# Row maxima turned on VectorE instead of TensorE, in a fused cross-attention and FP4 feed-forward kernel

## What is computed

```python
def reference(x, ctx_512, g_xattn, g_ffn, Wq, Wk, Wv, Wo, bo, w_gate, w_up, w_down):
    qh = (layernorm(x) @ Wq)      # (B, 16, N, 64)
    kh, vh = ctx_512 @ Wk, ctx_512 @ Wv
    attn = softmax(qh @ kh.T * 64 ** -0.5)
    x = x + tanh(g_xattn) * ((attn @ vh) @ Wo + bo)
    z = fp4(layernorm(x))
    h = silu(z @ fp4(w_gate).T) * (z @ fp4(w_up).T)
    return x + tanh(g_ffn) * (fp4(h) @ fp4(w_down).T)
```

## Time and profile before

| | us |
|---|---|
| median of 3 runs | 548.04 (547.64 to 551.53) |
| profiled execution | 547.66 |
| its span, first to last instruction | 545.8 |
| TensorE busy in it | 532.4 |
| VectorE busy | 439.2 |
| ScalarE busy | 312.8 |
| GpSimd busy | 279.9 |

### The profile page before, as it was taken

One profiled execution on the slowest core, in us unless ns is written; L12 is line 12 of the kernel. 1 busy time (PEld: TensorE's weight loads), 2 busy tenths in 40 slices (PEclk: granted clock), 3 DMA queues, 4 the chain that ended last, 5 costly groups with the idle time before them and its releaser, 6 DMA issues.

```text
span 545.8 us, 8243 instructions
## 1 busy us (share of the span) xinstructions
PE 532.4 (98%) x2769; PEld 319.8 (59%) x2769; DVE 439.2 (80%) x765; ACT 312.8 (57%) x724; POOL 279.9 (51%) x260
## 2 busy tenths in 40 slices
PE   7989999999999999999999999999999999999997
PEld 4655656656565665656566565756556565655553
DVE  5868889798887979798887978789786988877865
ACT  4365546765467556765467645665567654555611
POOL 4046294745629463574927465383826566184300
PEclk9999999999999999999999999999999999999999
DMA  7502001110012100020011100120000200000000
GB/s 186 114 1 56 0 1 31 29 27 2 1 34 37 19 1 28 9 55 0 2 29 35 28 0 2 36 54 1 1 28 4 29 1 1 5 0 1 2 4 4
DMA packets 10017, 12.28 MB, mean 23 GB/s; under 512 B 4144, under 2 KB 7736, under 8 KB 9976
## 3 DMA queue, kind: packets, MB, share of 16 engines
q1 hardware_dynamic: 9000, 8.85, 6.6%
q0 software_dynamic: 560, 2.59, 3.2%
q10 hardware_dynamic: 416, 0.33, 0.2%
HBM read 11.35 MB, written 0.41 MB: 22 GB/s over the span
## 4 chain that ended last, share of the span: by engine, by line
PE 91%; DVE 6%; issue 2%; ACT 1%; POOL 0%; DVEq 0%; ACTq 0%; POOLq 0%
PE attn L931 28%; PE scores L914 19%; PE ring L840 13%; PE scores L915 12%; PE ring L857 5%; PE ring L850 4%; PE ring L820 3%; DVE max L1071 2%; PE ring L863 2%; PE ring L871 1%; PE ring L843 1%; PE attn L887 1%; ACT q_hh L638 1%; DVE e_gate L1025 0%; PE ring L799 0%
## 5 line engine op out<-in xcount | busy, mean ns | idle before, releaser
L749 ACT ACTIVATE probs<-scores 120x400 f32<-120x400 f32 (+1 forms) x384 | 185.5, 505 | 158.5 <-PE scores L915 156.1
L1071 DVE TENSOR_REDUCE max<-ring 116x1 f32<-116x482 f32 (+2 forms) x336 | 203.5, 651 | 58.2 <-PE ring L840 56.7
L592 POOL TENSOR_TENSOR acc_p<-acc_p,probs 120x800 f32<-120x800 f32 x75 | 145.2, 1936 | 64.2 <-ACT probs L749 59.9
L931 PE MATMUL attn<-probs,ctx_n 120*64 120x400 f32 (+1 forms) x768 | 170.2, 524 | 0.6 <-ACT probs L749 0.6
L914 PE MATMUL scores<-q_hh,k_hl 128*120 128x400 f32 (+1 forms) x384 | 154.6, 402 | 1.2 <-DVE q_ls L1075 0.7
L914 PEld LDWEIGHTS scores<-q_hh,k_hl 128*120 128x120 f32 (+1 forms) x384 | 69.6, 181 | 125.1 <-ACT probs L749 89.5
L915 PE MATMUL scores<-q_ls,k_h 71*120 71x400 f32 (+1 forms) x384 | 133.0, 346 | 0.0
L840 PE MATMUL ring<-k_hl,q_hh 128*116 128x482 f32 (+2 forms) x336 | 111.9, 403 | 1.9 <-DVE q_ls L1053 0.7
L915 PEld LDWEIGHTS scores<-q_ls,k_h 71*120 71x120 f32 (+1 forms) x384 | 70.3, 183 | 3.8
L931 PEld LDWEIGHTS attn<-probs,ctx_n 120*64 120x64 f32 (+1 forms) x768 | 38.3, 134 | 53.6 <-issue 33.5
L840 PEld LDWEIGHTS ring<-k_hl,q_hh 128*116 128x116 f32 (+1 forms) x336 | 58.3, 178 | 12.1 <-DVE max L1071 3.0
(11 more groups left out here) (130 smaller groups left out, 473.4 us busy)
## 6 DMA issues: line engine op xcount, KB each, us to landing
ctx_n<-in_ctx SPq DMA_DIRECT2D x8, 360.0 KB
ctxT<-in_ctxT SPq DMA_DIRECT2D x7, 361.0 KB, 4.0
k_hl<-in_ctxT POOLq DMA_DIRECT2D x7, 361.0 KB, 5.0
wvT<-in_WvT SPq DMA_DIRECT2D x2, 256.0 KB, 4.5
wo<-in_L_xattn_Wo SPq DMA_DIRECT2D x1, 512.0 KB, 5.7
x_in<-in_x SPq DMA_DIRECT2D x8, 50.0 KB
out<-y_out SPq DMA_DIRECT2D x8, 50.0 KB
ctxT<-in_ctxT SPq DMA_DIRECT2D x2, 180.5 KB, 3.9
```

Of the source, the lines that this page charges most:

```text
L592: pool.tensor_tensor(acc_p[0:r, t.g % 2, :], left, probs[0:r, c % PROBS, :], ALU.add).then_inc(sum_p, 1)
L749: act.activation(probs[0:r, c % PROBS, k * HALF:(k + 1) * HALF], scores[0:r, slot % SCORE_BANKS, 0:HALF], ACT.Exp).then_inc(probs_full, 1)
L931: mm = pe.matmul(attn[64 * i:64 * i + C, k, 0:HALF], ctx_n[0:r, par, c, :], probs[0:r, c % PROBS, k * HALF:(k + 1) * HALF], start=(j == 0) ...
L1071: dve.tensor_reduce(max3[0:rows, tile, part:part + 1], src[0:rows, 0:MAXC[part + 1] - MAXC[part]], AX.X, ALU.max).then_inc(free, 1)
```

## The change

The shift matmul, its mask and the multiply go. `maxes` becomes 7 blocks of 32 columns, zero but for a diagonal: column t of block t holds tile t's maxima. VectorE transposes it in blocks of 32 by 32 (`turn_maxima`): four instructions, one for each quarter of the partitions, over the six whole tiles, and a fifth for the last 32 query rows, into `turned_max` at partitions 64 to 95. ScalarE copies 7 rows of it into `q_ls` (`shift_rows`); `k_h1` holds minus one there. For this the tiles are of 128 rows; the last begins at 800 - 128. The first q goes to a P·V bank instead of the ring, its splitting moves behind the start's maxima, all four vo tiles are made before group 0, and nearly all slot tables are new.

```diff
-TILES, TROWS = 7, 116
+TILES, TROWS, TURN = 7, 128, 32
+TROW = [min(t * TROWS, ROWS - TROWS) for t in range(TILES)]
+WHOLE = ROWS // TROWS
...
-MAX_TILES_SLOT = [19, 18]
-SHIFT_SLOT = [20, 20]
+MAX_TILES_SLOT = [16, 18]
+SHIFT_SLOT = [18, 21]
+TURN_COPY_SLOT = [22, 21]
...
-KLO_AT = 7
+KLO_AT = 8
...
-POOL_AT = {'ln1': 2, 'ln2': 6, 'swiglu': (1, 2, 4), 'heads': 5}
+POOL_AT = {'ln1': 2, 'ln2': 7, 'swiglu': (1, 2, 4), 'heads': 5}
...
-                pool.memset(k_h1[par][C:C + TILES, :].bitcast(F32), 1.0).then_inc(consts_set, 1)
+                pool.memset(k_h1[par][C:C + TILES, :].bitcast(F32), -1.0).then_inc(consts_set, 1)
...
+            def shift_rows(t, first, last, count):
+
+                act.wait_ge(turned, count)
+                act.activation(q_ls[C:C + TILES, (t.g + 1) % 2, first:last], turned_max[C:C + TILES, first:last], ACT.Copy).then_inc(shift_set, 1)
...
                 for slot in range(SLOTS):
                     exps(t, slot)
+                    if t.g == 0 and slot == FIRST_LATE_SLOT:
+                        shift_rows(t.before(), EARLY_TILES * TROWS, ROWS, 2)
+                    if slot == TURN_COPY_SLOT[t.g % 2] and t.g + 1 < GROUPS:
+                        shift_rows(t, 0, ROWS, t.count(1, 3))
...
-                elif kind in ("shift", "late"):
-                    pe.wait_ge(max_done, t.count(1, 3) if kind == "shift" and t.g >= 0 else t.count(1, 2))
-                    mm = pe.matmul(dst[C:C + TILES, 0:TROWS], maxes[0:TROWS, :], ident[0:TROWS, 0:TROWS], start=True, stop=True)
...
                 if slot == 0:
-                    wait_reads(pe, *[(t.before(), key) for key in (("q", 0), ("shift", 0))])
+                    pe.wait_ge(shift_set, t.count(1, 1 + (t.g > 0)))
...
-                elif kind == "shift":
-                    first, last = (0, TILES) if t.g >= 0 else (EARLY_TILES, TILES) if key[0] == "late" else (0, EARLY_TILES)
-                    n, cols = last - first, slice(first * TROWS, last * TROWS)
-                    dve.tensor_tensor(q_ls[C:C + TILES, (t.g + 1) % 2, cols].rearrange("p (k n) -> p k n", k=n), shift_mask[C:C + TILES, first:last, :],
-                                      src[C:C + TILES, 0:TROWS].rearrange("p (o n) -> p o n", o=1).to_broadcast([TILES, n, TROWS]), ALU.mult).then_inc(free, 1)
...
-                dve.tensor_reduce(maxes[0:TROWS, first:last], max3[0:TROWS, first:last, :], AX.X, ALU.max).then_inc(max_done, 1)
+                diagonal = maxes[:, :, :].rearrange("p k n -> p (k n)")[:, first * (TURN + 1):(last - 1) * (TURN + 1) + 1:TURN + 1]
+                dve.tensor_reduce(diagonal, max3[:, first:last, :], AX.X, ALU.max).then_inc(max_done, 1)
+
+            def turn_maxima(t, first, last, count):
+
+                whole = min(last, WHOLE)
+                dve.wait_ge(max_done, count)
+                if count > 2:
+                    dve.wait_ge(shift_set, count - 1)
+                for q in range(TROWS // TURN):
+                    rows = turned_max[C:C + TURN, first * TROWS:whole * TROWS].rearrange("p (k n) -> p k n", n=TROWS)[:, :, q * TURN:(q + 1) * TURN]
+                    op = dve.transpose(rows, maxes[q * TURN:(q + 1) * TURN, first:whole, :])
+                if last > WHOLE:
+                    op = dve.transpose(turned_max[C:C + TURN, WHOLE * TROWS:ROWS], maxes[TROWS - TURN:TROWS, WHOLE, :])
+                op.then_inc(turned, 1)
```

More of the change, by code:

```diff
@@ L853, in ring_use @@
                     if k == 0 and t.g == 1:
-                        wait_reads(pe, *[(Turn(-1 if part < 2 else 0), ("vo", part)) for part in range(4)], own=bank)
+                        wait_reads(pe, *[(Turn(-1), ("vo", part)) for part in range(4)], own=bank)
                     for i in range(4):
@@ L1046, in split_q @@
             def split_q(t, r):
-                half, (bank, n) = (t.g + 1) % 2, t.ring(("q", 0))
+                half = (t.g + 1) % 2
                 rows, cols = slice(64 * r, 64 * r + C), slice(r * HALF, (r + 1) * HALF)
-                if r == 0:
-                    dve.wait_ge(ring_full[bank], n)
+                if t.g < 0:
+                    src, read = attn[:, 0, :], first_q_read
+                else:
+                    bank, n = t.ring(("q", 0))
+                    src, read = ring[:, bank, :], ring_free[bank]
+                    if r == 0:
+                        dve.wait_ge(ring_full[bank], n)
                 dve.wait_ge(q_hi_done, t.count(4, 4 + 2 * r + 2))
-                op = dve.tensor_tensor(q_ls[0:C, half, cols], ring[rows, bank, 0:HALF], q_hh[rows, half, cols].bitcast(F32), ALU.subtract)
+                op = dve.tensor_tensor(q_ls[0:C, half, cols], src[rows, 0:HALF], q_hh[rows, half, cols].bitcast(F32), ALU.subtract)
+                if r == 0 and t.g < 0:
+                    op.then_inc(first_lo, 1)
                 if r == 1:
-                    op.then_inc(ring_free[bank], 1)
+                    op.then_inc(read, 1)
             def ring_use(t, key):
                 kind, k = key
-                if kind not in ("A", "max", "first", "shift", "late", "sum", "lsum", "down"):
+                if kind not in ("A", "max", "first", "sum", "lsum", "down"):
                     return
@@ L1062, in ring_use @@
                 src, free = ring[:, bank, :], ring_free[bank]
-                if kind in ("first", "late"):
-                    t, kind = t.before(), {"first": "max", "late": "shift"}[kind]
+                if kind == "first":
+                    t, kind = t.before(), "max"
                 dve.wait_ge(ring_full[bank], n)
```

159 lines of the change are left out of this document (88 added, 71 removed).

## The result

| us | before | after |
|---|---|---|
| median of 15 runs each | 547.65 (546.75 to 551.62) | 552.55 (550.34 to 553.01) |
| profiled execution | 547.66 | 552.56 |
| its span | 545.8 | 550.7 |
| granted clock, mean of the span | 1.000 | 0.993 |

The ratio is 1.0063, with an interval of 1.004 to 1.0085: the changed kernel is 0.6% slower. The prediction had 543.0, 538.2 to 548.3; the time lies 9.6 above it and outside its range. A run of either kernel also lists its clock. Runs listed with 0.998 or more are called runs at full clock. Some executions of the kernel before show less and are some 1 to 6 us longer; of the changed kernel all 15 do. That is part of the matter here.

The account below looks back on a forecast made before the run. TensorE was taken to bound the kernel by throughput, except around the shift matmul. Terms -2.1 - 0.5 + 2.7 + 0.6 - 1.1 - 1.3 - 2.9 = -4.6 took 547.66 to 543.0 us, range 538.2 to 548.3.

Parts of the forecast that it names:

- The shift matmul: Groups 1 to 14: removing it gains 0 in twelve groups, 2.1 us in groups 2 and 14 and the start.
- the hole: Slots 19 and 20: TensorE would wait there for ScalarE's exponential anyway, 1.21 us round trip against 0.83 of work.
- Rival A: The removed matmul gives its whole price in twelve groups, 4.6 us more gain: 538.4 us, chance 0.14.
- The x_hat transpose: Groups 2 to 12: its move from slot 18 into the hole gains six times 0.09, 0.5 us.
- Tiles of 128 rows: Maximum matmuls and VectorE's reductions, tiles formerly 116 and 104 rows: cost 0, at most 1.6 us in all.
- Transposes: VectorE, five a group, 1.35 us together, replacing a 1.0 us multiply: cost 0, covered by idle time.
- Rival D: VectorE's transposes wait for ports held by GpSimd's additions, and ScalarE and TensorE stall: 557 us, chance 0.08.
- The copy: ScalarE, one a group, 0.86 us long: free in odd groups, 0.34 in eight even ones, 2.7 us cost.
- The z chain: VectorE's z steps come later, z_fp4 just in time for slot 1; with the later key DMA, 0.6 us cost.
- Rival C: The key DMA comes 0.7 us too late in seven groups: 547.9 us, chance 0.12.
- The start: Before group 0: the first score comes at 19.8 instead of 20.93, gain 1.1 us (0.3 to 1.6).
- Group 0: Slots 0 to 5 gain 1.3 us, slots 6 to 23 gain 2.9; over 31 us would show the forecast wrong.

Follow-up runs that it names:

- e4_copy21: The changed kernel with ScalarE's copy of the turned maxima behind slot 21 in every group but the first; 552.17 us, ratio 1.0066.
- e6_order_old: The changed kernel with the z chain, GpSimd's LayerNorm step and the key DMA back at their old slots; 550.26 us, ratio 1.0029.
- e3_vo_late: The changed kernel with the first two vo tiles later, ahead of the eleventh maximum and behind the last one; 551.52 us, ratio 1.0056.
- e5_steady: e3_vo_late with three warming matmuls ahead of score 0, q's products moved to slot 5 and three warming matmuls ahead of them; 550.04 us, ratio 1.0024.
- e13_all_pv: e5_steady, e6_order_old and e4_copy21 together, three h links behind slot 21's transposes, two P·V pairs of group 0 one slot later; 545.26 us, ratio 0.9944.

## Why the prediction was wrong, step by step

The forecast was a gain of 4.6 us; the loss is 4.9. By its own steps:

1. The shift matmul, 0 in twelve groups, 2.1 in groups 2 and 14: this held. Groups 2 and 14 gave 0.92 and 0.49, and the copy took back 0.23 and 0.31 in them, so 1.15 and 0.80, some 1.9 together. In odd groups the hole stood open, with 0.23 of waiting in it. Rival A fell with it. The x_hat transpose that went into the hole in even groups cost nothing there: slots 19 and 20 take 1.22, and took 1.22 to 1.24. The 0.5 us that its move was to give did not arrive: slot 18 is 0.07 to 0.10 shorter, but group 4 without its last slot takes as long as before (30.70 for 30.71), so other slots took it.
2. Tiles of 128 rows: nothing seen, 0 as forecast.
3. Transposes: 0.370 where 0.3 stood, five in 1.68 where 1.35 stood, and never held up. Rival D's cause fell.
4. The copy: 0.87 long, 0.31 on the chain of nearly each even group (0.23 in group 2, 0.33 in group 0), where 0.86 and 0.34 stood. This held, and e4_copy21 took it away. What the step missed is that its price lay in series with the next one's.
5. **The z chain failed, by its size.** The text charged 0.1 us in six odd groups because "z_fp4 is ready just as slot 1 wants it". It is ready at 246.85, 2.71 behind the group's start, where it had been 2.33 (244.72 - 242.39). Slot 1 lost some 0.35 in five groups, 1.7, and e6_order_old gave it back. The step didn't ask which link of the chain would stand beside GpSimd's additions, and how many would be left behind it: L427 takes 2.6 us there, and two more links follow than in e6_order_old. The earlier trace rows show that such a step can take 2.47. In group 9 the same kind of step, ahead of the transposes, cost 1.1; nothing in the text allowed for it. Rival C's DMA came in time: the first maximum of the odd groups never waits for it.
6. **The start failed**: 20.94 where 19.8 stood. Maxima end at 18.66, not near 17.7, since the vo tiles among them hold TensorE, and transposes take 1.25 for 0.9 to 1.0. Moving the tiles alone gives about 0.85 (e3_vo_late and the starts compared there). Of the 1.1 some is chance: with the same instructions the first score varied by 1.1 us.
7. and 8. **Group 0 failed most**: 34.05 where 28.9 stood (7.7 + 20.9, and 0.34 for the copy at its end). The prediction's own sign of being wrong, group 0 over 31 us, came true, and at full clock too (31.90). Of the 5.1, 2.15 went when both idle stretches were filled (e5_steady), nearly all of it low clock: slots 0 to 5 alone lost 2.06. The clock stood in no term: no step priced the warming matmuls that the change takes out, or asked what a wait of 2 us does to the engine that waits. That filling the stretches decides is shown (full clock in none of 59 runs and in 24 of 29); that the removed warming matmuls by themselves would have held the clock is not. 0.6 is a P·V pair ahead of its own exponential, shown by e13_all_pv. The other 2.4 were in slots that were summed by prices with 0.5 left for stalls: in e5_steady slot 8's fourth maximum alone waits 0.68 for q's bank, and slots 3 to 5 run beside a VectorE that is busy 3.97 of 4 us from 22 to 26. The rest of it wasn't taken apart by a run.

Sum of the misses: start 1.1, group 0 5.1, odd groups' slot 1 beyond the 0.6 charged about 1.1, group 9 1.1, group 1 0.5 (31.11 for 30.62, not examined), the transpose of x_hat and small changes in the even groups 0.3: 9.2 of 9.6. More than half lies at the start, where the forecast had put more than its whole gain on a sum of prices, with a narrow range.

## What to carry to other kernels

A matmul that is taken away in a hole gives nothing, and what replaces it on another engine may stand on the chain: look which wait ends last there, and which comes next, since two waits in series give back what each alone seems to save. When instructions leave TensorE, look whether they, or the work beside them, covered an idle stretch of some 1.5 to 2 us: such a stretch costs its own length, and here it cost about as much again in clock (2.02 us of waiting, 2.06 us more in slots 0 to 5). Moving a small VectorE step is moving it against GpSimd's additions; price it with its long duration there, not with its median, and count the steps that are left when GpSimd is done. A profiled execution is one draw: the same start put the first score anywhere in 1.1 us and lost the clock at one place or another.
